# Rows of the first experts: kept by token and gathered by slot, in place of scattered by slot

## What is computed

```python
logits = x @ w_router                      # 32 experts, 4 choices per token
probs = softmax(logits); w_topk, sel = top_k(probs, 4)
pos = place of each choice in its expert, in order of tokens
valid = pos < 128                          # an expert takes its first 128 tokens
buf[e, pos] = x[tok]                       # rows by slot: 32 experts x 128 slots
y = (silu(buf @ w_gate) * (buf @ w_up)) @ w_down
out[tok] += y[e, pos] * w_topk * valid
sh = silu(x @ sw_gate) * (x @ sw_up) @ sw_down       # shared network, every token
out += sigmoid(x @ w_shared_gate) * sh
```

## Time and profile before

| | us |
|---|---|
| median of three runs (lowest, highest) | 1308.19 (1306.6, 1310.39) |
| the profiled execution | 1308.23 |
| its span, first to last instruction | 1306.4 |
| PE busy | 1086.5 (83%) |
| DVE busy | 962.8 (74%) |
| ACT busy | 893.6 (68%) |
| POOL busy | 702.6 (54%) |
| mean granted clock of TensorE | 0.936 |

### The profile page before, as it was taken

How to read it: one execution, slowest core, us unless ns; L and a number is a source line. 1 busy time by engine, 2 the same in 40 slices (tenths; PEclk the granted TensorE clock), 3 DMA queues, 4 the chain that set the end, 5 groups by cost and what they waited for, 6 DMA issues and landing times.

```text
span 1306.4 us, 23979 instructions
## 1 busy us (share of the span) xinstructions
PE 1086.5 (83%) x8185; PEld 634.8 (49%) x8300; DVE 962.8 (74%) x1787; ACT 893.6 (68%) x1533; POOL 702.6 (54%) x620
## 2 busy tenths in 40 slices
PE   6958888888888888888888768989988697798992
PEld 4623444444444444444444654556644254456771
DVE  6999899999999999999999564113345787642333
ACT  4649899999999999999999642124445466533441
POOL 3016988878888878887887437713330000452331
PEclk9969999999999999999999867989999898698997
DMA  5676788888888888888876391029853031123335
GB/s 172 126 140 140 152 171 160 162 175 166 166 184 160 160 181 166 167 180 163 161 149 106 58 278 60 19 58 275 257 190 133 1 82 51 42 83 92 100 95 208
DMA packets 393231, 182.50 MB, mean 140 GB/s; under 512 B 331376, under 2 KB 377045, under 8 KB 393112
## 3 DMA queue, kind: packets, MB, share of 16 engines
q1 hardware_dynamic: 384872, 164.30, 57.2%
q0 software_dynamic: 8016, 16.47, 3.6%
q10 hardware_dynamic: 224, 0.20, 0.1%
HBM read 52.70 MB, written 54.43 MB: 82 GB/s over the span
## 4 chain that ended last, share of the span: by engine, by line
PE 44%; DVE 31%; ACT 10%; issue 6%; DMA 5%; POOL 2%; SPq 1%; POOLq 0%; DVEq 0%; ACTq 0%
DVE top L368 20%; PE bank L217 8%; PE bank L231 7%; ACT weight L411 6%; PE bank L2267 4%; PE bank L1075 4%; PE bank L249 3%; DMA answered_rows<-yrow,target 3%; PE bank L1058 2%; PE bank L2283 2%; PE bank L1062 2%; PE bank L1435 2%; PE bank L1418 1%; PE bank L267 1%; DVE x_sb L1959 1%
## 5 line engine op out<-in xcount | busy, mean ns | idle before, releaser
L411 ACT ACTIVATE weight<-bank,bias,sq_all 128x1024 uint8<-128x1024 f32 x512 | 609.9, 1200 | 32.5 <-PE bank L231 27.1
L368 DVE TENSOR_REDUCE top<-bank 128x1 f32<-128x512 f32 (+1 forms) x683 | 610.8, 951 | 16.0 <-PE bank L217 4.7
L461 POOL CAST weight<-turned 128x2048 bf16<-128x2048 uint8 x256 | 478.8, 1892 | 43.5 <-PE bank L249 24.2
L231 PE MATMUL bank<-kT,query 128*128 128x512 bf16 x915 | 285.7, 384 | 26.3 <-ACT weight L411 12.1
L249 PEld LDWEIGHTS bank<-v_sb,weight 128*128 128x128 bf16 x4096 | 172.1, 97 | 109.8 <-POOL weight L461 7.5
L217 PE MATMUL bank<-kT,qspace 64*128 64x512 bf16 x687 | 138.2, 395 | 62.9 <-DVE top L368 62.9
L249 PE MATMUL bank<-v_sb,weight 128*128 128x16 bf16 x4096 | 172.7, 170 | 6.4 <-POOL weight L461 5.9
L217 PE MATMUL bank<-kT,query 128*128 128x512 bf16 x331 | 127.0, 384 | 2.1 <-DVE top L368 1.4
L1633 POOL DMA_INDIRECT dispatched_rows<-qspace,put x32 | 33.9, 1060 | 163.9 <-DVE qspace L2061 154.2
L231 PEld LDWEIGHTS bank<-kT,query 128*128 128x128 bf16 x1024 | 60.2, 97 | 104.2 <-ACT weight L411 60.9
L411 ACT ACTIVATION_READ_ACCUMULATOR weight<-bank,bias,sq_all 128x1 f32 x512 | 101.3, 198 | 0.0
(11 more groups left out here) (298 smaller groups left out, 1538.8 us busy)
## 6 DMA issues: line engine op xcount, KB each, us to landing
dispatched_rows<-zeros SPq DMA_DIRECT2D x32, 524.0 KB, 3.2
answered_rows<-zeros SPq DMA_DIRECT2D x16, 512.0 KB, 3.1
late<-answered_rows SPq DMA_DIRECT2D x16, 512.0 KB, 6.1
wgu<-in_L_ffn_w_gate SPq DMA_DIRECT2D x32, 176.0 KB
wgu<-in_L_ffn_w_up SPq DMA_DIRECT2D x32, 176.0 KB
wdn<-in_L_ffn_w_down SPq DMA_DIRECT2D x32, 176.0 KB
erow<-dispatched_rows SPq DMA_DIRECT2D x39, 131.0 KB, 2.1
dispatched_rows<-zeros SPq DMA_DIRECT2D x8, 536.0 KB, 3.1
```

Source lines behind the costliest of these rows:

```text
L231: mm = pe.matmul(unit[u % 2][:, v * 512:(v + 1) * 512], query2[:, t % 2, h, :], kT[:, h // 2, first + v * 512:first + (v + 1) * 512], star ...
L368: ve.tensor_reduce(top[:, first:first + count], bank[:, first % 3:first % 3 + count, :], AX.X, ALU.max).then_inc(s_max, 1)
L411: ac.activation(weight8[:, n % BYTES, u * 1024:(u + 1) * 1024], unit[u], ACT.Exp, bias=bias[:, n:n + 1], scale=sq_all[:, n:n + 1], accum_o ...
L461: po.tensor_copy(weight[:, n % 3, :, :, :].rearrange("p c q two -> p (c q two)"), turned8[:, n % 3, :, :].rearrange("p c q -> p (c q)").bi ...
```

## The change

The rows of all tokens are stored once, by token, into a table `kept` whose first 128 rows are zeros: four stores by SP, one per group. For each slot the row to take is found by matmuls: `mark_slots` compares each of a token's four places with the numbers 0 to 127, which gives one-hot matrices `marked` (token by slot), and scales `hot` by the tile's number plus one and by the token's lane; `fill_table` multiplies the two, 16 products per group, summed in bank 7 over all groups; `take_table` makes row numbers `source` of the sums. A place beyond 127 matches no slot, and an empty slot gets row 0. POOL gathers an expert's 128 rows by an indirect DMA (`gather_rows`), 32 in all, six ahead of use, between its scatters of answers. The limit, its sum and its cast leave `place`, and one matmul leaves `places`. The shared network of group 1 moves behind the first experts, and DVE's `combine(0)` stands behind its six chunks. SP spreads its loads of expert weights over the groups' stores. The second experts' row semaphores are replaced by ones that are in use already, with their counts.

```diff
-    dispatched = nc.dram_tensor("dispatched_rows", [E0 * CAP, ROW], F32).ap()
+    kept = nc.dram_tensor("kept_rows", [P + NTOK, ROW], F32).ap()
...
-    ZEROED = (E0 * CAP + NTOK * K0 + E1 * NTOK) // 512
+    ZEROED = (NTOK * K0 + E1 * NTOK) // 512 + 1
...
+            s_er1 = s_ew[0:RING]
...
-                for e in range(SLOTS):
+                for e in range(3):
                     load_expert(sp, e)
+                for g in range(NG):
+                    sp.wait_ge(sm_["destinations_ready"], g + 1)
+                    sp.dma_start(kept[P * (1 + g * G):P * (1 + (g + 1) * G), :].rearrange("(t p) c -> p t c", p=P),
+                                 rows0[:, g * G:(g + 1) * G, :]).then_inc(s_kept, 16)
+                    for e in range(3 + 2 * g, min(5 + 2 * g, SLOTS)):
+                        load_expert(sp, e)
...
-                po.wait_ge(s_zero, 16 * ZEROED)
-                for g in range(NG):
-                    po.wait_ge(sm_["destinations_ready"], g + 1)
-                    for t in tiles(g):
-                        for k in range(K0):
-                            po.indirect_dma_start(out=dispatched, out_offset=bass.IndirectOffsetOnAxis(ap=put[:, t, k:k + 1], axis=0),
...
+                po.wait_ge(s_ofree, NT)
+                po.iota(slot_n[:], pattern=[[1, P]], base=0, channel_multiplier=0).then_inc(sm_["slots_numbered"], 1)
...
-                    pe.matmul(at, every[:], number[:].unsqueeze(1).broadcast_to([P, G, E0]), start=True, stop=False)
+                    pe.matmul(at, before[:], mask[:, g * G:(g + 1) * G, :], start=True, stop=False)
...
+                def fill_table(g):
+                    pe.wait_ge(sm_["slots_marked"], g + 1)
+                    if g == 0:
+                        pe.wait_ge(sm_["projections_added"], 2 * NG)
+                    for n in range(G * K0):
+                        mm = pe.matmul(bank[:, 7, 0:2 * E0], marked[:, n, :], numbered[:, n, :, :].rearrange("p a e -> p (a e)"),
+                                       start=g == 0 and n == 0, stop=g == NG - 1 and n == G * K0 - 1)
+                    mm.then_inc(sm_["table_products"], 1)
...
                 places(2)
+                fill_table(0)
                 router(3)
+                fill_table(1)
                 places(3)
+                fill_table(2)
                 pe.wait_ge(s_wf, 64)
-                hidden0(0, 0, 6)
+                hidden0(0, 0, 1)
+                fill_table(3)
+                hidden0(0, 1, 6)
+                pe.wait_ge(sm_["rows_chosen"], 1)
                 answers0(0)
-                hidden0(1, 0, 6)
-                answers0(1)
...
-                    step(ve.tensor_tensor(ge[:], at, limit[:].unsqueeze(1).broadcast_to([P, G, E0]), ALU.is_ge))
-                    settle()
-                    ve.scalar_tensor_tensor(slot[:, g % 2, :, :].rearrange("p t e -> p (t e)"), ge[:].rearrange("p t e -> p (t e)"), FAR,
-                                            bank[:, 3, 0:G * E0], ALU.mult, ALU.add).then_inc(sm_["places_taken"], 1)
+                    ve.tensor_tensor(picked[:].rearrange("p (t k) e -> p t k e", k=K0), hot[:, g % 2, :, :].rearrange("p (t k) e -> p t k e", k=K0),
+                                     at.unsqueeze(2).broadcast_to([P, G, K0, E0]), ALU.mult).then_inc(sm_["places_taken"], 1)
...
+                def mark_slots(g):
+                    if g == 0:
+                        ve.wait_ge(sm_["slots_numbered"], 4)
+                    else:
+                        ve.wait_ge(sm_["table_products"], g)
+                    at = slots[:, g * G * K0:(g + 1) * G * K0]
+                    step(ve.tensor_tensor(marked[:], slot_b[:].unsqueeze(1).broadcast_to([P, G * K0, P]),
+                                          at.unsqueeze(2).broadcast_to([P, G * K0, P]), ALU.is_equal))
+                    for k in range(G):
+                        n = slice(k * K0, (k + 1) * K0)
+                        step(ve.tensor_scalar(numbered[:, n, 0, :], hot[:, g % 2, n, :], float(g * G + k + 1), None, ALU.mult))
+                    settle()
+                    ve.tensor_scalar(numbered[:, :, 1, :], hot[:, g % 2, :, :], lane[:, 0:1], None, ALU.mult).then_inc(sm_["slots_marked"], 1)
+
+                def take_table():
+                    ve.wait_ge(sm_["table_products"], NG)
+                    step(ve.tensor_scalar(tile_f[:], bank[:, 7, 0:E0], float(P), None, ALU.mult))
+                    settle()
+                    ve.tensor_tensor(source[:], tile_f[:], bank[:, 7, E0:2 * E0], ALU.add).then_inc(sm_["rows_chosen"], 1)
...
                 normalise(3)
+                mark_slots(0)
                 place(1)
                 choose(2)
+                mark_slots(1)
                 place(2)
                 choose(3)
+                mark_slots(2)
                 place(3)
+                mark_slots(3)
+                take_table()
                 hidden0(0, 0, 6)
                 answers0(0)
-                hidden0(1, 0, 6)
-                answers0(1)
...
-                    sp.dma_start(erow[:, e % RING, :], dispatched[e * P:(e + 1) * P, :]).then_inc(s_er[e % RING], 16)
+                    po.indirect_dma_start(out=erow[:, e % RING, :], out_offset=None, in_=kept,
+                                          in_offset=bass.IndirectOffsetOnAxis(ap=source[:, e:e + 1], axis=0), bounds_check=P + NTOK - 1,
+                                          oob_is_err=False).then_inc(s_er[e % RING], 16)
...
+                    po.wait_ge(s_kept, 16 * NG)
+                    po.wait_ge(s_zero, 16 * ZEROED)
+                    po.wait_ge(sm_["rows_chosen"], 1)
+                    for e in range(RING):
+                        gather_rows(po, e)
                     for e in range(E0):
+                        if e + RING < E0:
+                            gather_rows(po, e + RING)
                         po.wait_ge(sx_["targets_ready"], e + 1)
...
                         pe.wait_ge(sx_["answers_weighted"], E0)
+                        for c in range(NW0):
+                            hidden0(1, c)
+                        for k in range(G):
+                            answers0(1, k)
                         for c in range(NW0):
                             hidden0(2, c)
...
+                        for c in range(NW0):
+                            hidden0(1, c)
+                        combine(0)
+                        for k in range(G):
+                            answers0(1, k)
                         hidden0(2, 0)
                         hidden0(2, 1)
-                        combine(0)
                         hidden0(2, 2)
```

76 lines of the change are left out of this document (39 added, 37 removed).

## The result

The changed kernel takes 1301.0 us, the median of five runs (1300.13 to 1304.61), beside 1308.19 for the kernel before in the same batch (1304.83 to 1310.39). The ratio is 0.9954, 95% interval 0.9938 to 0.9969: 6.0 us by the ratio, 7.2 between the medians. A later batch repeated the changed kernel: 1300.18 against 1308.19, ratio 0.9940 (0.9924 to 0.9957). Two single executions of later runs (3387 us in again, 4895 us in early_chunks_again) count as slow, stay out of the ratios, and were not explained.

The account below looks back on a forecast made before the run. Attention kept DVE and ACT busy, then PE bound the shared network until the experts started. Front -22.9, warm start -3.0, gathers +1.0 and moved network +27.1 summed to +2.2: 1310.4 us, range 1302 to 1320.

Parts of the forecast that it names:

- The experts start at 844.8 instead of 867.65: -22.9 us: Front: marks and fills delay group 0's answers to 844.3, but group 1's network and the 2.9 us fetch go: -22.9 us.
- six gathers ... land by 825: Before the experts: six gathers, issued every 1.27 us from 814.5, land by 825, so the 2.9 us of fetching goes.
- Two products and the transposes warm save -3.0: Start of the experts: PE comes without a gap from 30 us of work, so first products run warm: -3.0 us.
- I take +1.0: Loaded experts: row fetches in POOL's queue beside scatters, bounds -8 and +16 us, taken as +1.0.
- Issue is free: Expert stage: POOL's two issues take 2.54 us per expert, below the period of 2.87, costing 0.3 us in all.
- the loop: Expert stage: a scatter's landing frees a row for DVE, PE, ACT and a later scatter; period (landing + 3.2)/3.
- +27.1 us: Last expert to group 2's answers: with group 1's network moved there, 60.4 us instead of 33.3, +27.1 us.
- the rest shifts whole: Behind group 2's answers: order and distances of ACT's scales stay the old ones, so no change, 0 us.
- The front stretches: Rival, front: PE idles more while DVE marks, clock stays low, or marks cost 1 us more: 1314 us; chance 0.11.
- The gather holds up the scatter: Rival, expert stage: fetches in POOL's queue delay scatters, +16 instead of +1: 1325 us, at half 1317; chance 0.19.
- The loop loosens: Rival, expert stage: scatters land sooner without fetches in SP's queue: 1301 us; chance 0.26 together with the other faster case.
- the faster cases: Rivals: expert stage at PE's pace, 1301 us; or marks at 2.75 plus half that loosening, 1303 us; together 0.26.

Follow-up runs that it names:

- again: The changed kernel once more, unaltered, on a chip with hold-ups: 1317.52 us, ratio 0.9702 to the kernel before.
- early_chunks_again: Changed kernel with two mark buffers and group 0's first two shared-network chunks in PE's idle stretches of the front, chip without hold-ups: 1293.31 us, ratio 0.9884 to before.
- marks_twice: Changed kernel with every comparison of mark_slots done twice: 1330.2 us, ratio 0.9787 to the kernel before, over two executions.
- two_marks: Changed kernel with two buffers for the marks in turn, so mark_slots(1) no longer waits for fill_table(0): 1315.65 us, ratio 0.9704 to the kernel before.
- gathers_only_again: Changed kernel with group 1's shared network back ahead of the experts, on a chip without hold-ups: 1309.41 us, ratio 1.0004 to the kernel before.
- the two runs with pauses: Changed kernel, second experts' dispatch waiting for landings before every fourth scatter: 1308.83 us; the same plus early chunks and two mark buffers: 1298.74 us.
- gathers_only: Changed kernel with group 1's shared network back ahead of the experts, on a chip with hold-ups: 1323.99 us, ratio 0.9759 to the kernel before.

## Why the prediction was wrong

- **"The experts start at 844.8 instead of 867.65: -22.9 us"**: this is the step that failed, by size and not by mechanism; the terms that were too dear are the marks, the fills, `choose` and `place`. Measured -28.6 and -29.2. By the first trace: three marks at 3.3 instead of 3.9 (-1.8), fills at 1.0 and 0.63 instead of 1.7 (fill 0 and 2 on the path, and fill 3: -2.4), `choose` and `place` shorter by 0.1 to 0.3 each (-0.8), the starting point 0.5 earlier; that is -5.5 of the 5.7. marks_twice shows that the three-fold count was right and two_marks that DVE's wait (3.0 forecast, 2.25 measured) was real. That fills cost what they do is read from the trace; no run varied them. I rounded each small term up, and five terms with the same sign make 6 us. The fill was priced from products of 128x128 at 0.11 us each; for 128x64 the trace has 1.01/16 = 0.06 at half clock.
- **"six gathers ... land by 825"**: right, they were issued from 809.7 to 816.5 and nobody waits for them. No fetch stands ahead of the experts.
- **"Two products and the transposes warm save -3.0"** and **"I take +1.0"**: together -2.0; the stage gained 0.8 and 4.2 us in the two traces of the changed kernel, 0.7 in gathers_only_again, 2.0 in early_chunks_again, and 1.2 and 3.2 in the two runs with pauses. The warm start is right: the first three experts' products come 2.8 us sooner. The +1.0 is near the mean of the traces by luck, for the reason given was wrong. "Issue is free" is the second step that failed: POOL's two issues take 2.74 and 2.93 us per expert where the chain stays on them for 27 and 20 us, not 2.54, and "the loop" over the landings, which was to set the period, carries half as much of the chain as before or less. The period came out nearly the same: scatters come every 3.00 and 2.85 us in the two traces, 2.93 before (the 6th to the 26th). Nor is a gather always early enough: the chain meets one that landed after 6.56 us (issued at 853.87) in the first trace, and two after 6.38 and 5.89 us (at 853.18 and 904.50) in the second. The 3 us of scatter between traces were not in the likeliest case.
- **"+27.1 us" behind the experts**: right, +27.3 in three traces, with the waits in their places.
- **"the rest shifts whole"**: it came 1.4 and 2.9 us shorter, at a higher granted clock.
- **Rivals.** "The front stretches" did not come. "The gather holds up the scatter" came in its mechanism, as told above, but without its price. The two had 0.30 of chance between them. "The loop loosens" came for 1.2 us beyond the warm start in one trace. None of my cases was a front that is simply 6 us shorter: the faster cases both hung on the comparison's mode or on the loop, so the range ended where the dear terms stopped. A case "all small terms at their lower ends" would have reached 1304, the expert stage's scatter (2.2 us below my -2.0 in one trace) 1302, and the last stage's 1.4 to 2.9 us the 1301 measured. My 3.3 us for three marks at 2.75 should have been 3.45, which changes nothing.
- On chips with hold-ups the same change is worth 3%, not 0.5%. No row of before could show that.

## What to carry to other kernels

A chain that passes the same helper three times counts every rounding three times: give the sum a lower end made of all the small terms at once, not only one for each mechanism. Transfers that are "hidden" can still cost: on some chips a dense stream of POOL's indirect DMAs delays the other engines' waits. Fewer issues were worth 33 us there (gathers_only); gaps of 2.3 us took the hold-ups out of the front as well, but the one run that had them was slower as a whole, and whether shorter pauses pay wasn't seen. A kernel should be timed on more than one chip before its stages are tuned. Where an engine idles between small steps, put independent work of the next stage there, as the two early chunks show: they took most of their own time out of the chain and kept the clock up.
